# A residual ring of three buffers instead of two, its reload queued one step later, and three engines' stages written out

## The reference

```python
# block 0, on sx = x
x = conv(sx, w_down, stride 2, padding 1, groups=256)      # 3x3, two channels in, one out: (8, 256, 64, 64)
labels = k_means(normalised x[0])                          # 256 channels into 8 clusters, 10 rounds, batch 0 only
v5 = mean of x over the channels of each cluster           # (8, 8, 64*64)
mu, var = gmm_fit(v5)                                      # per batch: 2 components, 10 EM rounds over 4096 pixels
gate = sigmoid(mu ordered by var, times w_conv)[labels]    # one number per batch and channel
up = repeat(gate * x + x, 2 channels) * w_up
y = bilinear_up_x2(up) + sx                                # back to (8, 512, 128, 128)
# block 1, on y
s = mean of y over the pixels                              # squeeze
shift = relu6(bn(w_fuse @ relu6(w_guide @ s)))             # excite: one number per batch and channel
out = y + shift
```

## Time and profile before

| | |
|---|---|
| median of 3 runs | 2568.73 us (2557.87 to 2576.21) |
| the profiled execution's own time | 2567.7 us |
| its span, first to last instruction | 2565.9 us |
| PE busy | 2189.4 us (85%), mean granted clock 0.888 |
| DVE, ACT, POOL busy | 1263.0, 1310.4, 705.5 us |
| moved by DMA | 808.43 MB, mean 315 GB/s |
| stages 0 and 1 with k-means | 0 to 481 us |
| stages 2 to 7 (convolution, EM, output) | 481 to 2189 us |
| stage 8 (EM, output), stage 9 (output) | 2189 to 2400, 2400 to 2566 us |

### The profile page before, as it was taken

One profiled execution on the slowest core, in us unless ns is written; L12 is line 12 of the kernel. 1 busy time (PEld: TensorE's weight loads), 2 busy tenths in 40 slices (PEclk: granted clock), 3 DMA queues, 4 the chain that ended last, 5 costly groups with the idle time before them and its releaser, 6 DMA issues.

```text
span 2565.9 us, 35348 instructions
## 1 busy us (share of the span) xinstructions
PE 2189.4 (85%) x10521; PEld 1300.6 (51%) x10521; DVE 1263.0 (49%) x3232; ACT 1310.4 (51%) x1710; POOL 705.5 (27%) x841
## 2 busy tenths in 40 slices
PE   8995699998999899988998899888998899655764
PEld 2355634554554556544564455445554455544653
DVE  0054343265535554465535554455535654677654
ACT  5531044565555555565555555555555555434554
POOL 0000011232323322332333322332322322333453
PEclk9995598999999888999899889998999989877887
DMA  6631144699999999999999999899989999877999
GB/s 248 240 120 66 66 174 166 240 359 352 351 356 351 343 362 359 356 348 346 362 376 338 344 345 361 339 347 348 344 334 358 350 358 361 345 293 285 383 425 402
DMA packets 109839, 808.43 MB, mean 315 GB/s; under 512 B 10880, under 2 KB 10880, under 8 KB 11392
## 3 DMA queue, kind: packets, MB, share of 16 engines
q1 hardware_dynamic: 75424, 542.34, 54.4%
q10 hardware_dynamic: 34272, 264.25, 27.5%
HBM read 538.12 MB, written 268.44 MB: 314 GB/s over the span
## 4 chain that ended last, share of the span: by engine, by line
PE 51%; DMA 31%; issue 5%; DVE 5%; POOL 2%; DVEq 2%; ACTq 1%; POOLq 1%; SPq 1%; ACT 0%
PE ps L679 26%; DMA out<-xres 21%; PE ps L877 12%; DMA xres<-x 6%; PE ps L690 4%; DMA xin<-x 3%; PE ps L824 2%; POOL interp L512 2%; PE ps L835 2%; DVE xres L1235 1%; DMA out<-xin 1%; PE ps L735 1%; ACTq L620 1%; DVEq L1239 1%; POOLq L504 1%
## 5 line engine op out<-in xcount | busy, mean ns | idle before, releaser
L679 PE MATMUL ps<-xin,taps 128*64 128x512 f32 (+1 forms) x4608 | 1100.1, 631 | 16.0 <-DMA xin<-x 13.8
L1235 DVE SCALAR_TENSOR_TENSOR xres<-ps,scale,xres 128x1024 f32<-128x1024 f32 (+2 forms) x672 | 591.9, 924 | 310.6 <-PE ps L877 249.4
L877 PE MATMUL ps<-interp,pairs 128*128 128x256 f32 (+1 forms) x2304 | 611.9, 432 | 120.7 <-POOL interp L512 91.0
L679 PEld LDWEIGHTS ps<-xin,taps 128*64 128x64 f32 x4608 | 336.3, 139 | 696.4 <-issue 684.0
L611 ACT ACTIVATE xres<-xres,shift 128x2048 f32<-128x2048 f32 x224 | 444.9, 1998 | 411.1 <-DMA xres<-x 408.6
L512 POOL TENSOR_TENSOR interp<-cst 128x2048 f32<-128x2048 f32 x128 | 462.2, 3611 | 661.3 <-PE ps L877 659.2
L877 PEld LDWEIGHTS ps<-interp,pairs 128*128 128x128 f32 x2304 | 505.6, 233 | 212.9 <-issue 64.8
L592 ACT ACTIVATE junk<-xin 128x2048 bf16<-128x2048 f32 x256 | 489.3, 1911 | 35.9 <-issue 25.8
L483 POOL TENSOR_TENSOR coef<-mu,ivar 128x16 f32<-128x16 f32 x80 | 17.7, 221 | 906.0 <-DVEq L923 906.0
L580 ACT ACTIVATE pairs<-ps 128x128 f32<-128x128 f32 x128 | 35.2, 275 | 311.1 <-PE ps L817 310.9
L583 ACT ACTIVATE pairs<-ps 128x512 f32<-128x512 f32 x256 | 140.1, 596 | 13.2 <-PE ps L824 10.3
(11 more groups left out here) (170 smaller groups left out, 1416.5 us busy)
## 6 DMA issues: line engine op xcount, KB each, us to landing
xin<-x ACTq DMA_DIRECT2D x126, 2048.0 KB, 14.9
xres<-x SPq DMA_DIRECT2D x224, 1024.0 KB, 10.3
out<-xres SPq DMA_DIRECT2D x224, 1024.0 KB, 13.9
xin<-x SPq DMA_DIRECT2D x32, 1024.0 KB, 14.1
out<-xin SPq DMA_DIRECT2D x32, 1024.0 KB, 11.0
xin<-x SPq DMA_DIRECT2D x2, 2048.0 KB, 11.9
cst<-consts SPq DMA_DIRECT2D x1, 412.0 KB, 3.0
wg<-w_guide SPq DMA_DIRECT2D x1, 256.0 KB, 12.9
```

What stands on the lines that cost most here:

```text
L679: mm = pe.matmul(half[:, :, 1:] if kx == 0 else half, taps[:, 2 * t + i, n, :], tap_input(h, i, ky, kx), start=n == 0, stop=n == len(TAPS) ...
L877: mm = pe.matmul(ps[:, PS_UP + pos // 4, (pos % 4) * W:(pos % 4 + n) * W], pairs[:, m, :], interp[:, pos:pos + n, :].rearrange("c r w -> c ...
L1235: m = dve.scalar_tensor_tensor(dst, up[:, pos * W:(pos + r1 - r0) * W], sc, dst, ALU.mult, ALU.add)
```

## The change

`xres` gets three buffers (`SLOTS = 3`; 16 KB more on each partition), and the buffer of an output step is o mod 3 instead of h. `residual()` now takes the number o of the output step alone, and gives buffer, semaphores and counts; from stage 8 on (`FULL` = 96) the ring is five: three `xres` and two `xin`. SP's program is one straight list for all 128 output steps: store o, then the reload of step o+2, which goes into the buffer of step o-1 and waits for the store of o-1. From step 97 on it is the reload of step o+4, into the buffer of step o-1 again. Since the buffer is now a Python number, ACT and DVE write all stages with output out, one step after the other, without hardware loops. PE and POOL keep theirs. The computation is the same.

```diff
+SLOTS = 3
-        xres = sb("xres", [P, 2, 2, XR, W])
+        xres = sb("xres", [P, SLOTS, 2, XR, W])
...
+        FULL = STEPS * (B - 2)
+
+        def residual(o, i):
+
+            n = o - FULL
+            if n < 0:
+                q, use = o % SLOTS, o // SLOTS
+            else:
+                q, use = n % (SLOTS + 2), n // (SLOTS + 2)
+                if q >= SLOTS:
+                    h = q - SLOTS
+                    return xin[:, h, i, 1:, :], spare_in[h][i], 16 * use + 16, spare_stored[h][i]
+                use += FULL // SLOTS
+            return xres[:, q, i, :, :], xres_in[q][i], 16 * use + 16, stored[q][i]
...
+            def reload(o):
                 for i in range(2):
-                    load_again(0, 0, h, h, i)
...
+                    tile, landed, count, freed = residual(o, i)
+                    if count > 16:
                         sp.wait_ge(freed, count - 16)
                     sp.dma_start(tile.rearrange("c r w -> c (r w)"),
+                                 dram_channel(xv, o // STEPS, o % STEPS // S, o % S, i)).then_inc(landed, 16)
...
+            END = B * STEPS
+            sp.wait_ge(km_done, 1)
+            for o in range(SLOTS):
+                reload(o)
+            for o in range(END):
+                if o == FULL:
+                    sp.wait_ge(conv_ps, B * STEPS)
+                    sp.wait_ge(xsummed, B * STEPS)
+                    sp.wait_ge(halo, B * STEPS)
+                    reload(o + SLOTS)
+                    reload(o + SLOTS + 1)
+                store(o)
+                ahead = SLOTS - 1 if o <= FULL else SLOTS + 1
+                if o > 0 and o + ahead < END:
+                    reload(o + ahead)
...
-                runs(do_em, act, round_, not do_conv, True)
+                runs(do_em, act, round_, do_out, True)
...
-            with act.Fori(1, B // 2 - 1) as jj:
-                for p in range(2):
-                    stage_body(2 * jj + p, p, True, True, True)
-            for p in range(2):
-                stage_body(B - 2 + p, p, True, True, True)
+            for j in range(2, B):
+                stage_body(j, j % 2, True, True, True)
...
-                runs(do_em, dve, round_, not do_conv)
+                runs(do_em, dve, round_, do_out)
...
-            with dve.Fori(1, B // 2) as jj:
-                for p in range(2):
-                    stage_body(2 * jj + p, p, True, True, True)
+            for j in range(2, B):
+                stage_body(j, j % 2, True, True, True)
```

More of the change, by code:

```diff
@@ L218, in build @@
         x_in = [sem(f"x_in{h}") for h in range(2)]
-        xres_in = [[sem(f"xres_in{h}{i}") for i in range(2)] for h in range(2)]
-        stored = [[sem(f"stored{h}{i}") for i in range(2)] for h in range(2)]
+        xres_in = [[sem(f"xres_in{q}{i}") for i in range(2)] for q in range(SLOTS)]
+        stored = [[sem(f"stored{q}{i}") for i in range(2)] for q in range(SLOTS)]
         spare_in = [[sem(f"spare_in{h}{i}") for i in range(2)] for h in range(2)]
@@ L377, in _ @@
             sp.dma_start(wd[:, :, :], w_down).then_inc(tables_in, 16)
-            def load_again(b, t, s, h, i):
-                sp.dma_start(xres[:, h, i, :, :].rearrange("c r w -> c (r w)"),
-                             dram_channel(xv, b, t, s, i)).then_inc(xres_in[h][i], 16)
             load(sp, 0, 0, 0, 0)
@@ L387, in _ @@
                 sp.dma_start(tile, src).then_inc(setup_in, 16)
[L389 to L413, removed]
@@ L415, in _ @@
-            sp.wait_ge(km_done, 1)
-            for h in range(2):
-                for i in range(2):
-                    load_again(0, 0, h, h, i)
-            with sp.Fori(1, B // 2 - 1) as jj:
-                for p in range(2):
[L421 to L432, removed]
+            def reload(o):
+                for i in range(2):
+                    tile, landed, count, freed = residual(o, i)
+                    if count > 16:
@@ L444, in _, with store @@
+            def store(o):
                 for i in range(2):
-                    tile, landed, count, freed = residual(j, t, u, h, i)
-                    sp.wait_ge(result[i], STEPS * (B - 2) + n + 1)
-                    sp.dma_start(dram_channel(ov, j - 2, t, 2 * u + h, i),
+                    tile, landed, count, freed = residual(o, i)
+                    sp.wait_ge(result[i], o + 1)
+                    sp.dma_start(dram_channel(ov, o // STEPS, o % STEPS // S, o % S, i),
                                  tile.rearrange("c r w -> c (r w)")).then_inc(freed, 16)
-                if 4 <= n + 3 < 2 * STEPS:
-                    tail_load(n + 3)
@@ L452, in _ @@
+            for o in range(END - SLOTS - 2, END):
                 for i in range(2):
-                    sp.wait_ge(stored[h][i], 16 * (B - 1) * STEPS // 2)
-                    sp.wait_ge(spare_stored[h][i], 16 * STEPS // 2)
+                    tile, landed, count, freed = residual(o, i)
+                    sp.wait_ge(freed, count)
         @block.gpsimd
@@ L1233, in step @@
                                 for r0, r1, pos in spans:
-                                    dst = residual(j, t, u, h, i)[0][:, r0:r1, :].rearrange("c r w -> c (r w)")
+                                    dst = residual(o, i)[0][:, r0:r1, :].rearrange("c r w -> c (r w)")
                                     m = dve.scalar_tensor_tensor(dst, up[:, pos * W:(pos + r1 - r0) * W],
```

## The result

The changed kernel takes 2427.36 us in the median (2417.22 to 2430.55, 4 runs), the kernel before, timed beside it, 2570.69 us. The ratio is 0.9442, 95% interval [0.9397, 0.9488]: 143 us less, where 74 were forecast. A ratio is taken here over those runs of a kernel that lie within 1.5% of its fastest; that leaves runs out in one case only, the kernel with three buffers in which SP waits for its own store. The profiled execution has a span of 2423.8 us, against 2565.9.

A forecast was written before the change was run, and what follows sets the result against it. SP's store and reload list and PE were taken to share the bound; -69 us in stages 3 to 7 and -5 in stage 9 make -74 from 2567.7, so 2494 us, range 2450 to 2540.

The forecast's parts named there:

- What bounded the kernel: Stages 3 to 7: SP's stores and reloads rule the first half of a stage, PE alone the second.
- Stage 9: Last stage, ruled by DMA: one more strip already loaded, 2.1 MB less to move at 426 GB/s, -5 us.
- the sum of a PE-ruled stage: Stages 3 to 7: PE-ruled steps add to 273.6 us against 287.4, a gain of 13.8 us a stage, 69 us together.
- the iterating step without the means: Seven steps of a stage without the block means, 16.8 us each as in stage 2, 117.6 us together.
- got no better: Iterating steps in the earlier trace rows had no stop for the ring, yet PE was no faster in them.
- PE gets better than its rows: Rival, 10%: PE keeps more of the 2.4 GHz clock, iterating steps 1.8 us shorter, 63 us more gained, 2431 us.
- Stage 2, put at 0: Stage 2, at 271 us, was already near the 273.6 us of PE-ruled steps, so no gain there.
- Writing out, put at 0 to 5 us: ACT loses register instructions and DVE loop ends, mostly off PE's chain: 0 to -5 us, taken as 0.
- DMA: Rival, 15%: with two queues filled the rate stays at 357 GB/s, a stage takes 282 us, the kernel 2536 us.
- The load of `xin`: More transfers in flight, but 6.8 us of cover for this load: cost 0, between 0 and 1 us a step.
- Fetching: Rival, 5%: longer instruction lists stop ACT, DVE and SP in some 40 blocks of 2.9 us, 116 us lost, 2610 us.
- could only help: By a Trainium skill page, straight code is fetched ahead and taken branches break this, so the change brings no loss.

The follow-up runs named there:

- the two last experiments: The changed kernel with eight extra ACT copies before the eviction in 18 steps, 2534.25 us; the changed kernel with mixture sums between the upsampling halves, 2361.73 us.
- experiment 398: The last experiment, 398 being its GB/s: the changed kernel with PE's mixture sums between the upsampling halves in iterating steps of stages 2 to 7, 2361.73 us.
- ACT's late eviction: The changed kernel with eight small extra ACT copies before it evicts the convolution, in 18 iterating steps of stages 2 to 7: 2534.25 us.

## Why the prediction was wrong

**What bounded the kernel: right.** The chain of stores through SP ruled part of each stage and PE the rest. Stages 3 to 7 lost their stops for the ring, and stage 8 stayed at 211. Stage 9 gave 5 us, as forecast, at the forecast's rate: 415 GB/s for 161 us are 66.8 MB, where 416 for 166 were 69.1. But its chain no longer runs through DMA, which the forecast did not see.

**The step that failed** is the sum of a PE-ruled stage, 273.6 us, which measured 260.8. It was made of steps that already held time at the lower clock. Ten stops of 0.8 us for the mixture sums are in the 273.6, so it has PE busy for 265.5 us, more than the 261.8 of the mean stage before, and the changed kernel has 251.2. The largest part is the iterating step without the means, which I took at 16.8 us and used seven times. The kernel before had a faster one as well, in the same stage 2, just ahead of the steps of the earlier trace rows:

```profile
509.80 0.27 PE L817 MATMUL ps<-cst,stage 128*128 128x128 f32 x1
...
524.80 0.27 PE L817 MATMUL ps<-cst,stage 128*128 128x128 f32 x1
...
536.25 3.71 PE L877 MATMUL ps<-interp,pairs 128*128 128x256 f32 x18
539.80 0.27 PE L817 MATMUL ps<-cst,stage 128*128 128x128 f32 x1
...
551.33 5.40 PE L877 MATMUL ps<-interp,pairs 128*128 128x256 f32 x18
```

Two steps of 15.0 us, then one of 16.8 that ends at 556.57, with no stop for the ring in any of them. In stages 3 to 7 of the changed kernel 24 of these 35 steps take 15.0 to 15.4 us and the others 16.7 to 17.0. By PE's first transposes the seven together are 109.1 us instead of 117.6. The three steps with the means are 57.1 instead of 59.7, the two starting steps 28.8 instead of 29.6, the four finishing ones 66.0 instead of 66.7. Stage 2 with its 271 us, the sum's measured neighbour, had 15.6 us of idle time in it. Two steps of the changed kernel on PE's timeline in stage 6:

```profile
1571.90 3.71 PE L845 MATMUL ps<-interp,pairs 128*128 128x256 f32 x18
1575.45 0.27 PE L785 MATMUL ps<-cst,stage 128*128 128x128 f32 x1
...
1632.26 5.40 PE L845 MATMUL ps<-interp,pairs 128*128 128x256 f32 x18
1637.50 0.27 PE L785 MATMUL ps<-cst,stage 128*128 128x128 f32 x1
```

The same 18 matmuls take 3.71 or 5.40 us. How often the slow ones come depends on the stops, as the two last experiments show from both sides: more stops, 0.92; fewer, 0.96. What a stop costs beyond its length does not follow from one number: by the kernels with more stops it is 0.4 to 0.65 of it, so the 16.0 us of stops that went from a stage would be worth 22 to 26 us, and 26.6 were measured. How a stop brings the lower clock is open too. It came right behind the stop of 3.43 us shown above, but in the kernel before PE stopped for 3.45 us ahead of 2028.26, and the convolution behind it took 8.32 us.

The forecast's sentence that a PE without stops "got no better" rested on the steps of the earlier trace rows, and the steps of 15.0 us beside them speak against it. The rival "PE gets better than its rows", priced at 2431 us and given 10%, is what happened. That its price is within 4 us is partly luck: its seven steps were to give 63 us and gave 5 x 8.5 = 43, and the other steps and stage 2 gave the rest.

**Stage 2, put at 0**, gave 7 us: it had waits for the ring too (between 590 and 625 us ACT waited four times for `xres`, 12.4 us in all). **Writing out, put at 0 to 5 us**, is worth 37 us with the old ring, on SP and not on the engines where I looked. In the changed kernel SP waits 1712 us for results, so there it should matter little; that kernel with SP in loops wasn't tried.

**DMA** was not the bound. The 357 GB/s of the best stage before was a rate set by waits, and became 390. The Trainium skill's page "DMA: Bandwidth & Descriptors", section "Where 436 GB/s comes from", says that about 358 GB/s on the HBM side binds; the windows of this kernel, with 378 to 390 and in the last experiment 398, do not agree. By the same page, in its section of measured sizes, each core gets roughly that much when both cores of an HBM domain stream, and here one core ran, so by that section the figure does not apply. **The load of `xin`** did not suffer (10.6 us instead of 15.6). **Fetching**: in stages 3 to 7 the longest of DVE's unexplained idle times is 0.5 us,

```profile
DVE part L1086 <- issue: 8.5, 50, 0.4
...
DVE ivar L890 <- issue: 0.9, 2, 0.5
```

and the page of the profile counts 81 fetches as before. That writing out "could only help" held for SP; for ACT and DVE alone it did not show.

## What to carry to other kernels

In a queue that both stores and reloads, look at what stands behind the wait: a reload that waits for the landing of the store just queued holds back the next store. Move the wait one step on and give the ring the buffer that this needs; here the buffer alone gave a quarter to a half of the 106 us of both, and the order alone lost 333. And when pricing a stop of PE, compare PE's busy time for the same matmuls between stages with many and few stops, and count the clock with the stop. Before a step's length goes into a sum, look at its neighbours in the trace: steps of the same work took 15.0 and 16.8 us there.

## What the runs showed of the hardware

With a store always awaited, stores landed in 14 to 16 us in the median and `xin` in 15 to 16; in the changed kernel in 7 and 11, at 9% more throughput, and the reloads took 10 to 11 in all of them. It is not the throughput that decides: with ACT's late eviction the rate in stages 3 to 7 is 359 GB/s, little above the 352 before, and there stores land in 5.5 us and `xin` in 10.0 (from 750 to 1900 us). Why the transfers fall into step in the first case was not taken apart. SP's issue of a reload and the next store in a loop, with numbers from registers, took 0.9 us more a step than with constants. Extra PE stops of 58 us brought 38 us of slower matmuls, with the clock down from 0.94 to 0.92, though the stop came from ACT and not from a transfer.
